# Queries and keys of a cross-attention layer transposed without padding and placed into the score operands by DMAs, in a program without a loop

## The chip, the cores and the metric

The kernel runs on one core of one Trainium2 chip. The metric is the device time of one execution in microseconds (us). A core has several engines, each with its own instruction queue: TensorE (PE in the profile, its weight loads PEld), VectorE (DVE), ScalarE (ACT), GpSimd (POOL) and SyncE (SP). Each works its own queue in order and waits for the others through semaphores. SP issues nearly all DMAs here.

## The reference

A batch has 128 tokens of width 256. Each of 16 batches goes through a cross attention with 32 heads of width 8 and a quantised feed-forward layer:

```python
x = x + xattn(layernorm(x), ctx, pos, pos, Wq, Wkv, Wout, bout)
x = x + ffn(layernorm(x), W1, b1, W2, b2, s_act1, s_act2)

q = (x @ Wq).reshape(b, n, 32, 8);  k, v = split(ctx @ Wkv)      # xattn
q, k = rope(q, pos), rope(k, ctx_pos)       # turns pairs (x1, x2) by angles
w = softmax(einsum('bqhd,bkhd->bhqk', q, k) / sqrt(8))
return einsum('bhqk,bkhd->bqhd', w, v).reshape(b, n, 256) @ Wout + bout
```

The feed-forward layer rounds its input, its weights and its hidden values (width 1024, after a ReLU) to 4 bits. The kernel keeps float32 accuracy in the scores by splitting a query or key into a rounded high part and a low rest; a score is then hi·hi + hi·lo + lo·hi, which are 24 rows of one contraction per head.

## The kernel before

The work is a software pipeline over batches. A *step* has eight *slots*, g = 0 to 7, and in step s stage n works on batch s - n: S_NORM (0), S_PROJ (1), S_STACK (2), S_MAX (3), S_ATT (4), S_OUT (5), S_FFN (6). There are 22 steps. The order of every engine's queue is written out by hand in its `body`. Steps 0 to 7 and 16 to 21 are straight code, and steps 8 to 15 are a loop of two steps. A slot of PE holds the scores of four heads for their maximum (`scores_for_max`, stage S_MAX), the scores of four heads of the batch before for the exponential (`scores_for_exp`, S_ATT), a weighing of values (`weigh_values`) and one or two other pieces of work, each in one of three shared PSUM banks (`ps_misc`; `claim` waits until the piece that had the bank before is emptied).

The part that the change touches:

- DVE multiplies the projected queries and keys by cosines and sines (`rope`, L796 and L801), and POOL adds the two into `rot` (L475).
- ACT writes the high part of each head twice into rows padded to 32 columns a head (`split_high`, L582: `q_rows`, `k_rows`), and POOL adds the low part (`split_low`, L483). The columns of four heads are 128 wide.
- PE transposes them four heads at a time, 8 + 8 transposes a batch in four pieces (`transpose_rows`: SQ0, SQ1, SK0, SK1), and ACT copies each piece out of PSUM, keys straight into `k_stack` (L601), queries into `q_comp` (L595).
- The queries of a group of four heads have to stand block-diagonally in `q_diag`: head j has its own rows and its own 128 columns, and the rest is zero. SP does this with four DMAs for each half of the groups (`place_queries`, L372).
- PE multiplies `k_stack` with `q_diag` in bf16 for the maxima. DVE reduces them (`maxima`, L810). PE transposes the maxima in two halves of 16 heads, DVE copies them to `mxT`, and SP places them in a row of `q_diag` that meets a row of -1 in `k_stack` (`place_maxima`, L380), so that the second scores, in float32r, come out with the maximum subtracted. First half in stage S_MAX, slot 4; second half in stage S_ATT, slot 1.

Both `k_stack` and `q_diag` have two buffers. `place_maxima`, `load_context` (L360) and `store` (L386, one store for two batches) stand in the same SP queue as `place_queries`.

## Time and profile before

| | |
|---|---|
| Time of an execution, median of 3 (lowest to highest) | 298.29 us (298.26 to 298.51) |
| Span of the profiled execution, first to last instruction | 296.1 us |
| PE busy | 250.3 us, 85% of the span, 2816 instructions |
| DVE busy | 223.3 us, 75% |
| ACT busy | 202.2 us, 68% |
| POOL busy | 128.1 us, 43% |
| Chain that ended last | PE 69%; issue 11%; DVE 10%; POOL 5%; ACT 4%; DMA 1% |
| Granted TensorE clock, mean | 0.943 of full speed |

The span is taken from one profiled execution, whose time as a whole is not listed; the median of the timed runs is 2.2 us above its span, which is what lies around the first and last instruction. The chain that ended last is followed back from the last instruction, at each step to what released it; "issue" is time in which the engine waited for nothing that the profile shows. Ends of matmuls are modelled, so that starts of neighbouring groups say more than their durations. DMA issues of SP are not counted as busy time, but the time that each held the queue is shown in a timeline of SP.

### The profile page before, as it was taken

The page shows a single profiled execution, that of the slowest core. Times are in us where ns is not written, and L with a number is a line of the kernel's source. Part 1 is how long each engine was busy: PE and PEld are TensorE (multiplying, and loading weights), DVE is VectorE, ACT ScalarE, POOL GpSimd, SP SyncE. Part 2 cuts the span into 40 slices and gives each one's busy share as a digit, 9 for nine tenths or more (in the row PEclk, how much of TensorE's full clock was granted, in tenths as well). Part 3 has the DMA queues.
Part 4 walks back from the last instruction along what each step waited for, and adds up shares of the span by engine and source line. Part 5 has one row for each costly group of instructions (what it writes and reads, how often), then busy time and mean ns, then how long its engine had stood idle before and what let it go on. Part 6 is the DMA issues. An engine that isn't in the chain of part 4 may idle for free.

```text
span 296.1 us, 8723 instructions
## 1 busy us (share of the span) xinstructions
PE 250.3 (85%) x2816; PEld 183.8 (62%) x2816; DVE 223.3 (75%) x570; ACT 202.2 (68%) x444; POOL 128.1 (43%) x266
## 2 busy tenths in 40 slices
PE   0056227899999999999999999999999999999653
PEld 0045126867767777777777777777777767665441
DVE  2977418797887979797979797979888877784441
ACT  3213025667679787878787878888887978679423
POOL 7625039444471717263635454445453451520110
PEclk9999557799999999999999999999999999999875
DMA  7921101252111113121211121112112111200101
GB/s 165 340 92 45 35 0 38 62 167 49 37 48 45 45 45 83 41 52 41 80 45 45 40 80 43 45 51 68 44 38 72 41 38 41 72 3 4 35 0 38
DMA packets 31786, 17.41 MB, mean 59 GB/s; under 512 B 6544, under 2 KB 31376, under 8 KB 31760
## 3 DMA queue, kind: packets, MB, share of 16 engines
q1 hardware_dynamic: 29696, 17.06, 21.8%
q10 hardware_dynamic: 2064, 0.02, 0.4%
q8 instruction: 15, 0.25, 0.3%
q14 instruction: 11, 0.09, 0.1%
HBM read 6.31 MB, written 2.10 MB: 28 GB/s over the span
## 4 chain that ended last, share of the span: by engine, by line
PE 69%; issue 11%; DVE 10%; POOL 5%; ACT 4%; DMA 1%; ACTq 0%; POOLq 0%; DVEq 0%
PE ps_misc L972 34%; PE ps_av L972 13%; PE ps_max L972 12%; PE ps_exp L972 9%; DVE turns L697 2%; ACT h_i L636 2%; DVE xn L867 1%; DMA q_diag<-mxT 1%; POOL rot L475 1%; DVE by_cos L796 1%; POOL q_rows L441 1%; DVE by_sin L801 1%; DVE xn L772 1%; POOL k_rows L442 1%; POOL rstd L515 1%
## 5 line engine op out<-in xcount | busy, mean ns | idle before, releaser
L810 DVE TENSOR_REDUCE mx<-ps_max 128x4 f32<-128x512 f32 x128 | 87.3, 686 | 30.0 <-PE ps_max L972 26.9
L607 ACT ACTIVATE expo<-ps_exp 128x512 f32<-128x512 f32 x128 | 77.7, 607 | 19.6 <-PE ps_exp L972 18.1
L972 PE MATMUL ps_exp<-q_diag,k_stack 128*128 128x512 f32 x128 | 60.3, 471 | 0.4 <-DMA q_diag<-mxT 0.4
L972 PE MATMUL ps_av<-expo,v_strip 128*32 128x128 f32 x1024 | 54.1, 285 | 0.0
L972 PE MATMUL ps_max<-k_stack,q_diag 96*128 96x128 bf16 (+1 forms) x512 | 52.9, 226 | 0.8 <-DVE mx L810 0.8
L636 ACT ACTIVATE h_i<-ps_misc,b1q,relu_scale 128x128 int16<-128x128 f32 x128 | 48.3, 470 | 2.5 <-PE ps_misc L972 2.5
L972 PEld LDWEIGHTS ps_max<-k_stack,q_diag 96*128 96x128 bf16 (+1 forms) x512 | 30.8, 99 | 24.5 <-issue 23.3
L500 POOL TENSOR_TENSOR v_strip<-v_comp,zeros 128x32 f32<-128x32 f32 x128 | 28.0, 256 | 19.4 <-PE ps_av L972 19.4
L972 PEld LDWEIGHTS ps_av<-expo,v_strip 128*32 128x32 f32 x1024 | 20.3, 108 | 21.8 <-issue 14.7
L483 POOL TENSOR_TENSOR q_rows<-rot,q_rows 128x256 f32<-128x256 f32 x16 | 11.6, 725 | 36.0 <-ACT q_rows L582 36.0
L972 PEld LDWEIGHTS ps_exp<-q_diag,k_stack 128*128 128x128 f32 x128 | 24.4, 190 | 1.5 <-issue 0.8
L468 POOL TENSOR_TENSOR rstd<-var,minus_half 128x1 f32<-128x1 f32 x16 | 8.9, 557 | 37.4 <-DVE var L766 37.4
L601 ACT CAST k_stack<-ps_misc 128x512 fp32r<-128x512 f32 x32 | 18.9, 590 | 8.6 <-PE ps_exp L972 5.3
L475 POOL TENSOR_TENSOR rot<-by_cos,by_sin 128x512 f32<-128x512 f32 x16 | 20.5, 1282 | 9.5 <-issue 6.9
L972 PE MATMUL ps_misc<-ident,q_rows 128*128 128x128 f32 x128 | 21.1, 291 | 1.8 <-POOL q_rows L483 1.8
L515 POOL TENSOR_TENSOR rstd<-var,minus_half 128x1 f32<-128x1 f32 x16 | 8.8, 549 | 30.8 <-DVE var L860 30.8
L595 ACT CAST q_comp<-ps_misc 128x512 fp32r<-128x512 f32 x32 | 19.1, 596 | 3.8 <-PE ps_misc L972 3.7
L972 PE MATMUL ps_misc<-xqT,w1T 128*128 128x128 bf16 x256 | 20.9, 229 | 0.7 <-ACT xqT L625 0.7
L972 PE MATMUL ps_misc<-ident,k_rows 128*128 128x128 f32 x128 | 19.9, 279 | 1.4 <-ACT v_comp L588 0.7
L972 PE MATMUL ps_misc<-w2T,hq 128*128 128x256 bf16 x128 | 17.7, 282 | 2.0 <-DVE hq L882 1.5
L483 POOL TENSOR_TENSOR k_rows<-rot,k_rows 128x256 f32<-128x256 f32 x16 | 11.7, 734 | 17.4 <-ACT k_rows L582 17.4
L582 ACT CAST q_rows<-rot 128x512 fp32r<-128x512 f32 x16 | 9.8, 613 | 13.1 <-POOL rot L475 13.1
(122 smaller groups left out, 514.3 us busy)
## 6 DMA issues: line engine op xcount, KB each, us to landing
q_diag<-q_comp SPq DMA_DIRECT2D x128, 64.0 KB, 2.0
w<-in_L_ffn_W_dram SPq DMA_DIRECT2D x2, 1024.0 KB, 8.2
...
q_diag<-mxT SPq DMA_DIRECT2D x32, 8.0 KB, 1.8
...
```

The source lines that it names most:

```text
L468: pool.tensor_tensor(rstd1[:, r, :], var1[:, r, :], minus_half[:, :], ALU.pow).then_inc(rstd1_ready, 1)
L475: pool.tensor_tensor(rot[:, r, :], by_cos[:, :], by_sin[:, :], ALU.add).then_inc(rot_ready, 1)
L483: pool.tensor_tensor(rows[:, r, :, at:at + HD], src, rows[:, r, :, 0:HD], ALU.subtract)\
L500: ins = pool.tensor_tensor(strips[:, s, :, 9 * s:9 * s + HD], vals, nothing, ALU.add)
L515: pool.tensor_tensor(rstd2[:, r, :], var2[:, r, :], minus_half[:, :], ALU.pow).then_inc(rstd2_ready, 1)
L582: act.copy(rows[:, :, 0:2, :] if n == 0 else rows[:, :, 0:3:2, :], src).then_inc(hi_ready, 1)
L595: act.copy(q_comp[:, r, 4 * half:4 * half + 4, :], src).then_inc(q_ready, 1)
L601: act.copy(k_stack[:, r, 4 * half:4 * half + 4, :], ps_misc[PIECE_BANK[(SK0, SK1)[half]]][:, :].rearrange("p (g t) -> p g t", g=4)).then_i ...
L607: act.activation(expo[:, g % EXPO, :], ps_exp[g % 2][:, :], ACT.Exp, scale=SCALE).then_inc(exp_done, 1)
L636: ins = act.activation(h_i[:, r, f, :], ps_misc[PIECE_BANK[(H0, H1)[half]]][:, 128 * c:128 * c + 128], ACT.Relu, bias=b1q[:, f:f + 1], sca ...
L810: dve.tensor_reduce(out=mx[:, r, 4 * g:4 * g + 4], in_=ps_max[g % 2][:, :].rearrange("p (h k) -> p h k", h=4), axis=AX.X, op=ALU.max).then ...
L972: return pe.matmul(out, lhsT, rhs, start=start, stop=stop, skip_group_check=True, **kw)
```

## The change

The queries and keys are no longer padded. The columns of Wq and of the key half of Wkv are reordered before the launch (`stack_order`), so that a transposed block of 128 columns of `rot` has its rows in the order that the score operands need. PE transposes `rot` itself, 4 transposes a batch in one piece (QKT) in slot 1. ACT writes the high part (`qk_hi`) and a full copy (`qk_full`), POOL subtracts (`qk_lo`). SP places everything: three DMAs for the keys and twelve for the queries, one for each part (high, high, low) and each of the four heads in a group. The operands have 96 rows in the order of the parts, and the row of maxima is row 96. `q_diag` and `k_stack` have three buffers; to make room, several tiles of the later stages reuse the memory of the unquantised weights (in the profile they are then called `w`). The DMAs of a batch count on one semaphore, `stacked`, and `scores_for_max` waits for all fifteen in slot 0.

The maxima are transposed and placed once a batch, in slot 0 of stage S_ATT. All later work, from `scores_for_exp` on, is three slots later (SHIFT = 3, `run_slots`; `st2` and `g2` are step and slot of that later part). The loop is gone: all 22 steps are straight code, with 3 slots more at the end. The order of the pieces and their banks is new. On DVE, `norm1` moves from slot `norm_at + 2` to `norm_at + 3`, and `rope` and `split_xT` to slots 4 and 3. POOL clears three buffers of `q_diag` in step 0.

```diff
-XT, SQ0, MX1, QK, SQ1, XQ, AT1, H0, SK0, MX0, AT2, VV, H1, WO, SK1, YY = range(16)
-PIECES = 16
-PIECE_BANK = (1, 2, 0, 1, 2, 0, 1, 0, 2, 1, 0, 2, 1, 0, 2, 0)
...
+MX, AT2, H1, WO, QKT, YY, XT, QK, XQ, AT1, H0, VV = range(12)
+PIECES = 12
+PIECE_BANK = (0, 1, 2) * 4
+SHIFT = 3
 EXPO = 4
...
+PART = 4 * HD
+NEG_ROW = 3 * PART
+STACK = 3
+PLACED = 16 * 15
 VREG = 3
...
+def run_slots(body):
+
+    for at in range(STEPS * GROUPS + SHIFT):
+        body(Step(at // GROUPS), at % GROUPS, Step((at - SHIFT) // GROUPS), (at - SHIFT) % GROUPS)
...
-        q_rows = sb("q_rows", [128, 2, HEADS, 32])
-        k_rows = sb("k_rows", [128, 2, HEADS, 32])
-        q_comp = sb("q_comp", [128, 2, GROUPS, 128], F32R)
-        k_stack = sb("k_stack", [128, 2, GROUPS, 128], F32R)
-        q_diag = sb("q_diag", [128, 2, GROUPS, 512], F32R)
+        qk_full = sb("qk_full", [128, 2, 2 * DIM])
+        qk_hi = sb("qk_hi", [128, 2, 2 * DIM], F32R)
+        qk_lo = sb("qk_lo", [128, 2, 2 * DIM], F32R)
+        k_stack = sb("k_stack", [128, STACK, GROUPS, 128], F32R)
+        q_diag = sb("q_diag", [128, STACK, 4, GROUPS, 128], F32R)
...
+            def stack_keys(st, part, rows):
+
+                at = st.ring(S_STACK, STACK)
+                dst = k_stack[PART * part:PART * part + PART, at, :, :].rearrange("p (g c) t -> p g (c t)", c=DC)
+                sp.dma_start(dst.bitcast(F32), rows[:, st.ring(S_STACK), DIM:2 * DIM].bitcast(F32)).then_inc(stacked[at], 16)
+
...
+            def spread_queries(st, part, rows):
+
+                at = st.ring(S_STACK, STACK)
                 for j in range(4):
...
+                    row = PART * part + HD * j
+                    dst = q_diag[row:row + HD, at, j, :, :].rearrange("p (g c) t -> p g (c t)", c=DC)
+                    src = rows[PART * j:PART * j + PART, st.ring(S_STACK), 0:DIM]
+                    sp.dma_start(dst.bitcast(F32), src.bitcast(F32)).then_inc(stacked[at], 16)
...
+            def stack(st):
+
+                st.wait(sp, qk_hi_ready, S_STACK, 1, 1)
+                st.wait(sp, exp_scores, S_STACK, GROUPS, GROUPS - STACK * GROUPS)
+                if st.s == S_STACK:
+                    sp.wait_ge(zeros_ready, 3)
+                stack_keys(st, 0, qk_hi)
+                stack_keys(st, 2, qk_hi)
+                spread_queries(st, 0, qk_hi)
+                spread_queries(st, 1, qk_hi)
+                st.wait(sp, qk_lo_ready, S_STACK, 1, 1)
+                stack_keys(st, 1, qk_lo)
+                spread_queries(st, 2, qk_lo)
+
+            def place_maxima(st):
+
+                at = st.ring(S_ATT, STACK)
+                st.wait(sp, mxT_ready, S_ATT, 1, 1)
+                dst = q_diag[NEG_ROW:NEG_ROW + 1, at, :, :, :].rearrange("o j g t -> o (j g) t")
+                sp.dma_start(dst.bitcast(F32), mxT[:, st.ring(S_ATT), :].bitcast(F32)).then_inc(neg_placed[at], 16)
 
             def store(st):
 
                 st.wait(sp, y_ready, S_FFN, 1, 1)
-                pair = st.value(1, (st.s - S_FFN) // 2)
+                pair = st.batch(S_FFN) // 2
                 sp.dma_start(out_pairs[pair], y[:, :, :]).then_inc(stored, 16)
...
+                if st.has(S_ATT):
+                    place_maxima(st)
                 if st.has(S_NORM) and st.s > 1:
                     load_context(st)
-                if not st.looped and st.s in (2, 4):
+                if st.s in (2, 4):
                     load(3 if st.s == 2 else 4)
-                if st.has(S_ATT):
-                    place_maxima(st, 1, S_ATT)
                 if st.has(S_STACK):
-                    place_queries(st, 0)
-                if st.has(S_MAX):
...
-            def split_low(st, n):
-
-                r = st.ring(S_PROJ)
-                rows, at = (q_rows, k_rows)[n], (16, 8)[n]
-                st.wait(pool, hi_ready, S_PROJ, 2, n + 1)
-                src = rot[:, r, n * DIM:(n + 1) * DIM].rearrange("p (h d) -> p h d", d=HD)
-                pool.tensor_tensor(rows[:, r, :, at:at + HD], src, rows[:, r, :, 0:HD], ALU.subtract)\
-                    .then_inc(lo_ready, 1)
+            def split_low(st):
+
+                r = st.ring(S_STACK)
+                st.wait(pool, qk_full_ready, S_STACK, 1, 1)
+                st.wait(pool, qk_hi_ready, S_STACK, 1, 1)
+                wait_stacked(pool, st)
+                pool.tensor_tensor(qk_lo[:, r, :], qk_full[:, r, :], qk_hi[:, r, :].bitcast(F32), ALU.subtract)\
+                    .then_inc(qk_lo_ready, 1)
 
...
+                prev = Step(st.s - 1)
+                if st.has(S_STACK):
+                    split_low(st)
+                if prev.has(S_OUT):
+                    norm2(prev)
+                    if prev.s == S_OUT:
+                        pool.wait_ge(bias_ready, 2)
...
+                    for r in range(STACK):
+                        clear_diagonal(r)
...
-                act.copy(q_comp[:, r, 4 * half:4 * half + 4, :], src).then_inc(q_ready, 1)
-
-            def copy_keys(st, half):
+                st.wait(act, qkT_in_psum, S_STACK, 1, 1)
+                wait_stacked(act, st)
+                act.copy(qk_hi[:, r, :], ps_misc[PIECE_BANK[QKT]][:, :]).then_inc(qk_hi_ready, 1)
+
+            def copy_qk(st):
                 r = st.ring(S_STACK)
-                st.wait(act, k_in_psum, S_STACK, 2, half + 1)
-                st.wait(act, exp_scores, S_STACK, GROUPS, 4 * half + 4 - 2 * GROUPS)
-                act.copy(k_stack[:, r, 4 * half:4 * half + 4, :],
-                         ps_misc[PIECE_BANK[(SK0, SK1)[half]]][:, :].rearrange("p (g t) -> p g t", g=4)).then_inc(k_ready, 1)
+                st.wait(act, qk_lo_ready, S_STACK, 1, -1)
+                act.copy(qk_full[:, r, :], ps_misc[PIECE_BANK[QKT]][:, :]).then_inc(qk_full_ready, 1)
...
+                cos_b = bcast(bcast(cos8[:, b, :, :].rearrange("p f c -> p (f c)"), 1, 2 * GROUPS), 3, 4)
+                dve.tensor_tensor(by_cos[:, :].rearrange("p (g d j) -> p g d j", d=HD, j=4),
+                                  ps.rearrange("p (g d j) -> p g d j", d=HD, j=4), cos_b, ALU.mult).then_inc(rope_terms, 1)
...
+                if g == norm_at + 3 and st.has(S_NORM):
+                    norm1(st)
...
-            def transpose_rows(st, piece, rows, in_psum, ready, half):
-                ps, r = claim(st, piece), st.ring(S_STACK)
-                st.wait(pe, lo_ready, S_STACK, 2, ready)
-                for g in range(4):
-                    h = 4 * (4 * half + g)
-                    ins = transpose(ps[:, 128 * g:128 * g + 128], rows[:, r, h:h + 4, :].rearrange("p h c -> p (h c)"),
-                                    ident[:, :])
-                ins.then_inc(in_psum, 1)
+            def transpose_qk(st):
+                ps, r = claim(st, QKT), st.ring(S_STACK)
+                st.wait(pe, rot_ready, S_STACK, 1, 1)
+                for n in range(4):
+                    ins = transpose(ps[:, 128 * n:128 * n + 128], rot[:, r, 128 * n:128 * n + 128], ident[:, :])
...
             def scores_for_max(st, g):
 
-                r = st.ring(S_MAX)
-                if g % 4 == 0:
-                    st.wait_dma(pe, diag_placed[g // 4], S_MAX, 64)
-                    st.wait(pe, k_ready, S_MAX, 2, g // 4 + 1)
+                at = st.ring(S_MAX, STACK)
+                if g == 0:
+                    st.wait_dma(pe, stacked, S_MAX, PLACED)
                 st.wait(pe, max_done, S_MAX, GROUPS, g - 1)
...
-            def transpose_maxima(st, half, stage, piece):
-                ps, r = claim(st, piece), st.ring(stage)
-                st.wait(pe, max_done, stage, GROUPS, 4 * half + 4)
-                transpose(ps[0:16, 0:128], mx[:, r, 16 * half:16 * half + 16], ident[:, :]).then_inc(mx_in_psum, 1)
+            def transpose_maxima(st):
+                ps, r = claim(st, MX), st.ring(S_ATT)
+                st.wait(pe, max_done, S_ATT, GROUPS, GROUPS)
+                transpose(ps[0:HEADS, 0:128], mx[:, r, :, :].rearrange("p j g -> p (j g)"), ident[:, :]).then_inc(mx_in_psum, 1)
 
             def scores_for_exp(st, g):
 
-                r = st.ring(S_ATT)
-                if g % 4 == 0:
-                    st.wait_dma(pe, neg_placed[g // 4], S_ATT, 16)
+                at, rows = st.ring(S_ATT, STACK), slice(0, NEG_ROW + 1)
+                if g == 0:
...
+                if g == 0 and st.has(S_ATT):
+                    transpose_maxima(st)
+                if g2 == 5 and st2.has(S_OUT):
+                    transpose_attn(st2)
+                if g2 == 6 and st2.has(S_OUT):
+                    project_out(st2)
+                if g == 3 and st.has(S_PROJ):
+                    transpose_x(st)
+                if g2 == 3 and st2.has(S_OUT):
+                    transpose_av(st2)
+                if st2.has(S_ATT):
+                    scores_for_exp(st2, g2)
+                if g2 == 5 and st2.has(S_FFN):
+                    hidden(st2, 1, H1)
...
+def stack_order(name, a):
+
+    if name == 'L0_xattn_Wq':
+        return a.reshape(DIM, 4, DC, 4, HD).transpose(0, 2, 3, 4, 1).reshape(DIM, DIM)
+    if name == 'L0_xattn_Wkv':
+        keys = a[:, :DIM].reshape(CTX, 4, DC, 4, HD).transpose(0, 2, 3, 4, 1).reshape(CTX, DIM)
+        return np.concatenate([keys, a[:, DIM:]], axis=1)
+    return a
 
```

The queue of SP. Before, one step of the straight part (step 7). `mxT` are the maxima, and `out_dram` is the output:

```order
L380 DMA q_diag<-mxT 1x16x128 [waits mxT_ready]
L372 DMA q_diag<-q_comp 32x4x128 [waits exp_scores,q_ready]
L372 DMA q_diag<-q_comp 32x4x128 x3
L380 DMA q_diag<-mxT 1x16x128 [waits mxT_ready]
L372 DMA q_diag<-q_comp 32x4x128 [waits exp_scores,q_ready]
L372 DMA q_diag<-q_comp 32x4x128 x3
L386 DMA out_dram<-y 128x2x256 [waits y_ready]
```

The same place of SP's queue in the changed kernel, step 7 and behind it the first instruction of step 8:

```order
L377 DMA q_diag<-mxT 1x32x128 [waits mxT_ready]
L341 DMA c_in<-in_ctx_dram 128x128 [waits xT_in_psum]
L347 DMA k_stack<-qk_hi 32x4x256 [waits exp_scores,qk_hi_ready]
L347 DMA k_stack<-qk_hi 32x4x256
L356 DMA q_diag<-qk_hi 8x4x256 x8
L347 DMA k_stack<-qk_lo 32x4x256 [waits qk_lo_ready]
L356 DMA q_diag<-qk_lo 8x4x256 x4
L383 DMA out_dram<-w 128x2x256 [waits y_ready]
L377 DMA q_diag<-mxT 1x32x128 [waits mxT_ready]
```

Fifteen DMAs stand where eight stood, and the maxima of the next step come right behind the store.

PE before, slot 4 of step 7:

```order
L972 MATMUL ps_max<-k_stack,q_diag 128x128 [waits max_done,k_ready,diag_placed_hi0]
L972 MATMUL ps_max<-k_stack,q_diag 128x128 x3
L972 MATMUL ps_misc<-ident,k_rows 128x128 [waits lo_ready,q_ready]
L972 MATMUL ps_misc<-ident,k_rows 128x128 x3
L972 MATMUL ps_exp<-q_diag,k_stack 128x512 [waits exp_done,neg_placed_hi1]
L972 MATMUL ps_misc<-ident,mx 16x128 [waits max_done,attn_ready]
L972 MATMUL ps_av<-expo,v_strip 32x128 [waits exp_done]
L972 MATMUL ps_av<-expo,v_strip 32x128 x3
```

PE in the changed kernel, slot 0 of a step, with the wait for the fifteen DMAs at its head:

```order
L935 MATMUL ps_max<-k_stack,q_diag 128x128 [waits max_done,stacked2]
L935 MATMUL ps_max<-k_stack,q_diag 128x128 x3
L935 MATMUL ps_misc<-ident,mx 32x128 [waits max_done,attn_ready]
L935 MATMUL ps_misc<-ident,attn 128x128 [waits attn_ready,relu_done]
L935 MATMUL ps_misc<-ident,attn 128x128
L935 MATMUL ps_exp<-q_diag,k_stack 128x512 [waits exp_done]
L935 MATMUL ps_misc<-xqT,w1T 128x128 [waits xqT_ready,v_copied]
L935 MATMUL ps_misc<-xqT,w1T 128x128 x7
```

PE in the changed kernel, from the last product of the feed-forward layer in slot 2 (`w2T`) to the first scores of the next batch for the exponential in slot 3, which wait for the placed maxima:

```order
L935 MATMUL ps_misc<-w2T,w 128x256 [waits hq_ready]
L935 MATMUL ps_misc<-w2T,w 128x256 x3
L935 MATMUL ps_av<-expo,v_strip 32x128 [waits exp_done]
L935 MATMUL ps_av<-expo,v_strip 32x128 x3
L935 MATMUL ps_max<-k_stack,q_diag 128x128 [waits max_done]
L935 MATMUL ps_max<-k_stack,q_diag 128x128 x3
L935 MATMUL ps_misc<-ident,xn 128x128 [waits c_loaded0,xn_ready,x2_ready]
L935 MATMUL ps_misc<-ident,xn 128x128
L935 MATMUL ps_misc<-ident,c_in 128x128
L935 MATMUL ps_exp<-q_diag,k_stack 128x512 [waits exp_done,neg_placed0]
```

Before, the last product of a batch stood in slot 7 and the placed maxima were waited for in slots 0 and 4; now these two stand in neighbouring slots.

## Rows read from the trace of the kernel before

**Rows 1.** Windows: length, busy us (x instructions) by engine, PEclk, DMA share, GB/s.

```profile
24.00:43.00 19.00, 6.71 (x38) 5.03 (x36) 8.63 (x15) 3.79 (x8) 4.73 (x13) 0.67 0.13 31
...
103.29:218.75 115.46, 115.46 (x1394) 86.02 (x1393) 99.00 (x264) 96.05 (x217) 55.02 (x121) 1.00 0.21 52
```

**Rows 2.** Timeline of PE, slots 4 to 7 of step 7: start, us, what.

```profile
103.13 0.60 PE L972 MATMUL ps_misc<-ident,k_rows 128*128 128x128 f32 x4
103.48 0.48 PE L972 MATMUL ps_exp<-q_diag,k_stack 128*128 128x512 f32 x1
103.80 0.27 PE L972 MATMUL ps_misc<-ident,mx 128*16 128x128 f32 x1
104.01 0.43 PE L972 MATMUL ps_av<-expo,v_strip 128*32 128x128 f32 x8
104.36 0.41 PE L972 MATMUL ps_max<-k_stack,q_diag 96*128 96x128 bf16 x4
...
105.06 0.28 PE L972 MATMUL ps_misc<-wkv_hi,xT_hi 128*128 128x256 f32 x1
...
105.41 0.62 PE L972 MATMUL ps_misc<-xqT,w1T 128*128 128x128 bf16 x8
106.32 0.41 PE L972 MATMUL ps_max<-k_stack,q_diag 96*128 96x128 bf16 x4
...
107.55 0.60 PE L972 MATMUL ps_misc<-ident,k_rows 128*128 128x128 f32 x4
108.07 0.43 PE L972 MATMUL ps_av<-expo,v_strip 128*32 128x128 f32 x8
108.43 0.41 PE L972 MATMUL ps_max<-k_stack,q_diag 96*128 96x128 bf16 x4
108.65 0.48 PE L972 MATMUL ps_exp<-q_diag,k_stack 128*128 128x512 f32 x1
108.97 1.05 PE L972 MATMUL ps_misc<-w2T,hq 128*128 128x256 bf16 x8
...
110.31 0.41 PE L972 MATMUL ps_max<-k_stack,q_diag 96*128 96x128 bf16 x4
```

**Rows 3.** Timeline of PE, first scores of steps 4, 17 and 18.

```profile
55.18 1.06 PE L972 MATMUL ps_max<-k_stack,q_diag 96*128 96x128 bf16 x8
...
240.21 0.41 PE L972 MATMUL ps_max<-k_stack,q_diag 96*128 96x128 bf16 x4
...
253.57 0.41 PE L972 MATMUL ps_max<-k_stack,q_diag 96*128 96x128 bf16 x4
...
265.00 0.49 PE L972 MATMUL ps_exp<-q_diag,k_stack 128*128 128x512 f32 x1
```

**Rows 4.** Timeline of SP: start, us that the issues held the queue, what.

```profile
24.93 5.29 SPq L372 DMA_DIRECT2D q_diag<-q_comp  x8
30.27 0.59 SPq L360 DMA_DIRECT2D c_in<-in_ctx_dram  x1
...
109.21 2.54 SPq L372 DMA_DIRECT2D q_diag<-q_comp  x4
111.79 0.59 SPq L386 DMA_DIRECT2D out_dram<-y  x1
113.05 0.35 SPq L360 DMA_DIRECT2D c_in<-in_ctx_dram  x1
```

**Rows 5.** Instructions on the tile q_diag: duration ns min/median/max, first and last start.

```profile
L380 SPq DMA_DIRECT2D q_diag<-mxT x32: 502/569/602, 53.1 to 267.1; - x32
...
DMA to landing us min/median/max: 1.8/2.0/3.7
```

**Rows 6.** The page's costliest groups: ACT's copy of four transposes, mean ns.

```profile
L595 ACT CAST q_comp<-ps_misc 128x512 fp32r<-128x512 f32 x32 | 19.1, 596 | 3.8 <-PE ps_misc L972 3.7
```

**Rows 7.** Groups by line: DVE's output of a batch.

```profile
L889 DVE SCALAR_TENSOR_TENSOR y<-ps_misc,h_scale,x_b 128x256 f32<-128x256 f32 x16 | 7.8, 484 | 4.6 <-PE ps_misc L972 3.9
```

**Rows 8.** Timeline of all engines: POOL's rotation of batch 1.

```profile
40.06 1.25 POOL L475 TENSOR_TENSOR rot<-by_cos,by_sin 128x512 f32<-128x512 f32 x1 [6.89 <-issue]
```

492 lines of the change are left out of this document (193 added, 299 removed).

## Prediction

> **What bounds the kernel now.** I read the page's shares first. PE is busy for 85% of the span, and holds 69% of the chain that ended last; the span's ends are where it is not busy. The windows then show that in the middle it is busy without a gap: 115.46 of 115.46 us, at the full clock, against 99.00 for DVE and 96.05 for ACT [rows 1]. Eight steps begin alike there, and a step lasts (240.21 - 110.31) / 9 = 14.43 us [rows 2, 3]. So what PE no longer does is gained, until another engine or a queue needs more than a step. DVE needs 99.00 / 8 = 12.4 us of a step and ACT 12.0. The engine that counts as nothing in these views is SP. Its timeline [rows 4] shows that four placing DMAs hold its queue for 2.54 us, and that the next issue begins 2.58 us after the first: 0.645 us for each. Eight of them cost 5.2 us of a step, in two halves, and PE never waits for one.
>
> **PE's work per step.** Twelve transposes go. Four take 103.48 - 103.13 = 0.35 us in one place and 108.07 - 107.55 = 0.52 in another [rows 2], 0.11 us each in the mean: -1.3 us. One of two transposes of maxima goes (104.01 - 103.80 = 0.21). The rest is moved, not changed: the contraction of the scores gets 96 or 97 rows instead of 96 or 128, and the number of columns that stream through is the same. PE would need 14.43 - 1.3 - 0.2 = 12.9 us. DVE loses one copy and keeps about 12.2, and ACT loses six passes of about 0.6 us [rows 6] for two. If nothing else came up, the nine full steps alone would bring 14 us.
>
> **Loop, shift, set-up.** The loop's turns leave no gap in [rows 1], so I take nothing for removing it. The three slots at the end are without scores for the maxima; they cost 4.6 us, as worked out below. POOL clears two more buffers in step 0, and saves the padding; its rotation of batch 0 waits for DVE anyway. I put nothing for both.
>
> **The queue of SP is what I expect to set the time.** Follow a step of the changed kernel from its first scores, T. Slot 0 holds what slot 5 held (104.36 to 106.32, 1.96 us [rows 2]) without the values' projection (105.41 - 105.06 = 0.35) and with the maxima (0.21): 1.82 us. Slot 1 holds exactly the pieces of the old slot 6, whose transposes ended 108.07 - 106.32 = 1.75 after its start: the four transposes end at T + 3.57, and slot 2 begins at T + 3.93 (slot 6: 2.11). ACT has its exponential behind it, copies `qk_hi` in 0.6 us [rows 6] and is done at about T + 4.3. SP waits also for the last exponential scores of three batches back, which stand in slot 2: they start at T + 3.93 + (108.65 - 108.43 = 0.22) and take 0.48 [rows 2]. So the first of fifteen DMAs is issued at T + 4.65. The low part, which the last five need, comes from ACT's second copy (T + 4.9) and a POOL pass of 1.25 us like the rotation [rows 8], at T + 6.2, well before its turn.
>
> The price of an issue: the trace of before has no transfer of these shapes. The nearest rows are 0.645 us for 32 x 4 x 128 [rows 4] and 0.569 + 0.04 = 0.61 for the small transfer of the maxima [rows 5], which moves an eighth of the bytes: the size hardly matters. Between them I take 0.645 for the three key DMAs and 0.62 for the twelve of queries. The last issue then begins 3 x 0.645 + 11 x 0.62 = 8.8 us after the first, and lands 2.0 us later [rows 5]. That is T + 4.65 + 8.8 + 2.0 = T + 15.45. PE waits for all fifteen at the head of the next step, and needed only 12.9 us to come there. It stands still for 2.5 us, and the next step's transposes begin after that: the delay is not absorbed, it is the period. The third buffer does not help, because transposes, DMAs and first use lie in two neighbouring steps. The bounds: above, 0.66 us for an issue, as in the first eight (30.27 - 24.93 = 5.34 [rows 4]), which makes a step 16.0 us. Below, 0.35 + 0.04 us, as the context's load when nothing is just ahead of it [rows 4]; the fifteenth then lands at T + 12.1 and is hidden.
>
> The Trainium skill speaks against this price: "DMA: Bandwidth & Descriptors", section "Anatomy of one DMA — SWDGE (gpsimd) path" (written for DMAs that GpSimd issues), puts the sequencer's dispatch at about 50 ns and most of a DMA's 2 us behind the last byte, and the section "Issuing engines are not separate DMA queues" calls the time to initiate a DMA usually small. By its 50 ns all fifteen would land at about T + 7.4. The trace disagrees with 0.645 us of queue for each, and I go by the trace; landing in 2.0 us agrees.
>
> **The store's wait, every second step.** The store of two batches waits for y. Its last product is now in slot 2 of the next step: it starts at T + 3.93 + 0.54 and takes 1.05 us, DVE's output 0.48 [rows 7], so y is ready at T + 6.1. Queued behind the store on SP are the maxima (wanted by PE in slot 3, at about T + 6.3), the context, and all fifteen DMAs. Store, maxima and context take 3 x 0.62 = 1.9 us (the store 0.59 [rows 4]). The maxima are issued at T + 6.7 and land 1.8 us later [rows 5], at T + 8.5: PE waits 2.2 us in slot 3. The first of fifteen is issued at T + 8.0 instead of T + 4.65, so the step lasts 8.0 + 8.8 + 2.0 = 18.8 us; the stall in slot 3 disappears in that. The stores of steps 7, 9, 11, 13 and 15 do this to steps 8, 10, 12, 14 and 16.
>
> **The sum.** Batch 1 is rotated until 41.3 us [rows 8]. DVE now does its rope after scaling the weights, which I give up to 2 us, and transposes and copy at the low clock take 1.2: its DMAs start at 44.5 and land at 55.3, when step 4 begins (55.6 before, the second half of the eight in [rows 3]). Steps 4, 5 and 6 have fewer pieces ahead of the transposes: without exponential scores, feed-forward and output projection I take 2.7, 3.2 and 4.1 us in place of 4.65. With 10.8 each, step 7 begins at 97.7. One step of 15.45: step 8 at 113.1 (110.3 before). One of 18.8: step 9 at 131.9. Four pairs of 34.25: step 17 at 268.9 (240.2 before [rows 3]). One of 15.45: step 18 at 284.4 (253.6 before). Step 18 has no transposes and no stacking but waits 2.2 us for the maxima behind the last such store: 13.3 us, to 297.7 (265.0 before). From there the old kernel took 296.1 - 265.0 = 31.1 us, and the new one adds the three slots: 1.82 + 2.11 + 1.88 - 3 x 0.22 - 0.52 = 4.6. The span is 333.4 us. With the 2.2 us that lie around it (298.29 - 296.1) the time is 335.6 us: 12% slower.
>
> **Rivals.**
> - *The issues are cheap and the fifteen DMAs are hidden* (the skill's rule, or the 0.35 us of [rows 4]). For it speaks that the transfers of queries have only 32 runs each, a quarter of before, and that the DMA engines are busy for 0.21 of the time [rows 1]. Against it: the transfer of the maxima has even fewer and held the queue for 0.569 us in the median of 32. A step is then 12.9 us, and the step after a store 14.6 to 14.8, because the maxima behind the store remain late (1.8 us of landing after T + 6.1). Steps 4 to 8 come 3 to 7 us earlier, the pair lasts 27.5 us for 28.9, and the three slots cost 4.6: 290 us, to 294 at 0.39 us for an issue. This is the other side: it turns at about 0.43 us for an issue, above which the pair with the store costs more than is gained.
> - *Only the fifteen DMAs delay, the store's wait costs nothing*: if y were ready before SP is through, all steps would last 15.45 us. Five steps lose 3.35 us less and step 18 2.2: 335.6 - 19 = 317 us. The order of the instructions speaks against it, since SP is through with step 7 at T + 4.65 + 9.4 = T + 14.1, before y's step begins.
> - *DVE or POOL becomes the bound* when PE sheds work: DVE's 12.2 us are below 12.9, and its waits for PE would shrink. It could make 13.2 us of 12.9, and matters only beside the first rival.
> - *The clock falls* in the new gaps. It was 0.67 where PE worked for 6.71 of 19.00 us [rows 1]; here it would work for 12.9 of 15.45. At the lower of its two levels (1.2 instead of 2.4 GHz) PE would be the bound again at up to 25 us a step, above 400 us.
>
> **Chances and range.** The forecast has 0.69, the cheap issues 0.14 (split into 0.12 faster and 0.02 within the bound), the free store 0.14, the clock 0.03. About 0.2% is what a measurement of this kernel can tell from no change; only the first rival reaches there. So faster 0.12, same 0.02, slower 0.86. For the forecast alone: issues of 0.60 to 0.66 us move a step by 0.3 us down and 0.6 us up, 14 steps by 4 and 8 us; a start of the DMAs 0.4 us earlier or later does 6; a landing up to 0.4 us later another 6. That is 322 to 348. The range reaches down to 311 to hold the second rival and leaves out the first.
>
> **What would show it.** PE's scores for the maxima (`ps_max`) wait for a DMA of `q_diag` or `k_stack` once a step, about 2.5 us after steps without a store and about 3.7 us at the end of those behind a store (18.8 less the 15.1 that PE needs with its stall in slot 3). The chain that ended last shifts from PE to SP's issues and landing DMAs. SP's timeline shows fifteen issues in 9.4 us. `ps_exp` waits for the maxima's DMA in steps 8, 10, ... by about 2 us. Transposes of `rot` are 64 in all, in place of 256. The steps alternate near 15.4 and 18.8 us. The forecast is wrong if an issue holds SP's queue for 0.4 us or less, or if first scores don't wait for DMAs; the sum is wrong in size if the start of the fifteen lies elsewhere than 4.65 and 8.0 us into a step.

## The result: 31% slower, and the profile after

| | before | after | forecast |
|---|---|---|---|
| median, us | 298.4 (298.3 to 300.1, 4 runs) | 392.8 (389.8 to 395.9, 4 runs) | 335 (311 to 348) |
| span of the profiled execution, us | 296.1 | 389.2 | 333.4 |
| PE busy | 85% | 69% | |

The ratio of the times is 1.313 (95% interval 1.304 to 1.321); it leaves out the run of 395.9 us, and every ratio below leaves out runs that lie more than 1.5% above the fastest of the same kernel, while the medians hold all runs. The direction was forecast, the time lies far above the range. First the page of the changed kernel: PE's share of the span, the granted clock in 40 slices, and the chain that ended last.

```profile
PE 267.8 (69%) x2608; PEld 190.4 (49%) x2608; DVE 227.5 (58%) x554; ACT 174.0 (45%) x380; POOL 127.1 (33%) x249
...
PEclk9999995887978887898698788968896889689995
...
SPq 39%; PE 26%; issue 12%; DMA 11%; DVE 8%; POOL 3%; ACT 1%; ACTq 0%; POOLq 0%; DVEq 0%
```

SP's queue leads the chain with 39%, where PE had 69% before. New is the third row: the clock is no longer full in the middle (1.00 in [rows 1]), and is 0.851 in the mean. The waits say who waits for whom (total, times, longest, in us):

```profile
PE ps_max L935 <- DMA q_diag<-qk_lo: 54.7, 15, 6.0
...
PE ps_exp L935 <- DMA q_diag<-mxT: 14.9, 6, 3.5
```

Both waits are the forecast ones: first scores for the maxima wait 15 times for the last query DMAs, and exponential scores 6 times for the maxima behind a store. Now one step without a store ahead of it, in which PE's two ends are 174.50 - 156.09 = 18.41 us apart (15.45 forecast). PE first:

```profile
156.09 0.40 PE L935 MATMUL ps_max<-k_stack,q_diag 96*128 96x128 bf16 x4 [1.95 <-DMA q_diag<-qk_lo]
...
159.18 0.41 PE L935 MATMUL ps_misc<-wout_hi,attnT_hi 128*128 128x256 f32 x1
...
160.46 0.66 PE L935 MATMUL ps_misc<-ident,rot 128*128 128x128 f32 x4
...
174.50 0.61 PE L935 MATMUL ps_max<-k_stack,q_diag 96*128 96x128 bf16 x4 [3.64 <-DMA q_diag<-qk_lo]
```

Then SP's queue in the same step (start, how long the issues held it):

```profile
162.17 1.24 SPq L347 DMA_DIRECT2D k_stack<-qk_hi  x2
163.46 5.83 SPq L356 DMA_DIRECT2D q_diag<-qk_hi  x8
169.33 0.59 SPq L347 DMA_DIRECT2D k_stack<-qk_lo  x1
169.96 2.81 SPq L356 DMA_DIRECT2D q_diag<-qk_lo  x4
```

The first of fifteen is issued at T + 6.08 (4.65 forecast), the last one at about 172.1, 9.93 us after it (8.8 forecast), and PE starts on it 2.4 us later (2.0 forecast). The sum 6.08 + 9.93 + 2.4 is the step. The row at 159.18 tells why the start is late: this product of 128x256 takes 0.41 us where the same form takes 0.28 at full clock [rows 2]. The first scores behind the stall still have the duration of full clock (0.40 us at 156.09); PE's clock then stood at the lower of its two levels from about 157.6 us until the transposes began at 160.46. Over the whole step the granted clock was 0.90, and over the next one 0.77.

The next step stands behind a store and takes 195.85 - 174.50 = 21.35 us (18.8 forecast):

```profile
181.83 0.40 SPq L383 DMA_DIRECT2D out_dram<-w  x1
182.27 0.57 SPq L377 DMA_DIRECT2D q_diag<-mxT  x1
182.89 0.58 SPq L341 DMA_DIRECT2D c_in<-in_ctx_dram  x1
183.58 1.25 SPq L347 DMA_DIRECT2D k_stack<-qk_hi  x2
```

```profile
184.45 0.80 PE L935 MATMUL ps_exp<-q_diag,k_stack 97*128 97x512 f32 x1 [2.15 <-DMA q_diag<-mxT]
...
195.85 0.40 PE L935 MATMUL ps_max<-k_stack,q_diag 96*128 96x128 bf16 x4 [1.49 <-DMA q_diag<-qk_lo]
```

Store, maxima, context and stack stand in the order that was forecast, and the stall in slot 3 has the forecast size (2.15 for 2.2). That the sizes agree so well is partly luck: the store held the queue for less than forecast (0.44 us to the next issue, for 0.62), and the maxima took longer to land (2.1 us in the median, for 1.8). The start is at T + 9.08 in place of 8.0. A pair of steps lasts 39.76 us where 34.25 were forecast.

The start is late too. Step 4 begins at 62.65 instead of 55.3, and most of that comes from a place at which I had put nothing. DVE, then POOL:

```profile
7.95 11.54 DVE L663 CAST red<-turns 128x64 f32<-128x64 int32 x1
19.52 0.23 DVE L664 SCALAR_TENSOR_TENSOR red<-red,ang 128x64 f32<-128x64 f32 x1
```

```profile
9.02 10.42 POOL L439 MEMSET q_diag<- 128x4096 int32 x3
```

A conversion of 64 columns that takes 0.20 us elsewhere shows 11.54 us. It begins beside POOL's subtraction for `wkv_lo` (7.82 to 9.08) and ends as POOL's three clears end. The first norm is behind the rope tables now.

### The profile page after: what moved, and what is told of

It reads as the page before. It is cut to its first block, busy times and chain, and to the rows that moved or that the text cites. A ratio compares the mean times of both kernels' runs of the same rounds, so it can differ in the third digit from the quotient of the medians.

```text
span 389.2 us, 7534 instructions
## 1 busy us (share of the span) xinstructions
PE 267.8 (69%) x2608; PEld 190.4 (49%) x2608; DVE 227.5 (58%) x554; ACT 174.0 (45%) x380; POOL 127.1 (33%) x249
## 2 busy tenths in 40 slices
DMA packets 27701, 21.74 MB, mean 56 GB/s; under 512 B 6544, under 2 KB 27280, under 8 KB 27664
## 4 chain that ended last, share of the span: by engine, by line
SPq 39%; PE 26%; issue 12%; DMA 11%; DVE 8%; POOL 3%; ACT 1%; ACTq 0%; POOLq 0%; DVEq 0%
SPq L356 29%; PE ps_misc L935 13%; DMA q_diag<-qk_lo 9%; SPq L347 7%; PE ps_max L935 5%; PE ps_exp L935 4%; PE ps_av L935 4%; DVE red L663 3%; SPq L377 1%; DMA pos_sb<-in_fside_BxSx_dram 1%; DVE w L856 1%; SPq L341 1%; DMA q_diag<-mxT 1%; SPq L383 1%; DVE w_i L698 1%
## 5 line engine op out<-in xcount | busy, mean ns | idle before, releaser
L935 PE MATMUL ps_max<-k_stack,q_diag 96*128 96x128 bf16 x512 | 59.4, 247 | 56.5 <-DMA q_diag<-qk_lo 54.7
L935 PE MATMUL ps_exp<-q_diag,k_stack 97*128 97x512 f32 x128 | 69.4, 542 | 14.9 <-DMA q_diag<-mxT 14.9
L935 PEld LDWEIGHTS ps_max<-k_stack,q_diag 96*128 96x128 bf16 x512 | 34.9, 108 | 86.0 <-DMA q_diag<-qk_lo 58.6
L469 POOL TENSOR_TENSOR qk_lo<-qk_full,qk_hi 128x512 fp32r<-128x512 f32 x16 | 20.3, 1272 | 129.0 <-ACT qk_full L575 129.0
L609 ACT ACTIVATE w<-ps_misc,b1q,relu_scale 128x128 int16<-128x128 f32 x128 | 48.0, 461 | 4.9 <-PE ps_misc L935 4.8
L935 PEld LDWEIGHTS ps_exp<-q_diag,k_stack 97*128 97x128 f32 x128 | 28.7, 224 | 17.5 <-DMA q_diag<-mxT 16.3
L935 PEld LDWEIGHTS ps_misc<-xqT,w1T 128*128 128x128 bf16 x256 | 19.0, 118 | 7.0 <-issue 5.4
L935 PE MATMUL ps_misc<-w2T,w 128*128 128x256 bf16 x128 | 17.6, 283 | 2.7 <-ACT w L609 2.7
L935 PEld LDWEIGHTS ps_misc<-w2T,w 128*128 128x128 bf16 x128 | 11.6, 101 | 6.7 <-ACT w L609 3.1
L935 PE MATMUL ps_misc<-ident,rot 128*128 128x128 f32 x64 | 12.5, 330 | 2.8 <-POOL rot L461 2.8
```

Source lines behind the costliest of these rows:

```text
L469: pool.tensor_tensor(qk_lo[:, r, :], qk_full[:, r, :], qk_hi[:, r, :].bitcast(F32), ALU.subtract)\
L609: ins = act.activation(h_i[:, r, f, :], ps_misc[PIECE_BANK[(H0, H1)[half]]][:, 128 * c:128 * c + 128], ACT.Relu, bias=b1q[:, f:f + 1], sca ...
L935: return pe.matmul(out, lhsT, rhs, start=start, stop=stop, skip_group_check=True, **kw)
```

## The experiments

Step lengths below are read from PE's first scores, as above. "Before" ran beside every kernel, at 297.8 to 298.8 us.

| kernel (no ratio where a part of the work is left out) | us, median (4 to 10 runs) | ratio to before |
|---|---|---|
| changed kernel | 392.8 | 1.313 |
| store behind the next stacking | 375.5 | 1.260 [1.256, 1.264] |
| half the bytes | 387.3 (380.9 to 391.1) | |
| eleven DMAs | 341.0 (337.3 to 345.0) | |
| PE kept busy | 373.7 | 1.256 [1.249, 1.263] |
| spread clears | 391.2 | 1.312 [1.308, 1.317] |
| late store, busy PE, spread clears | 348.8 | 1.173 [1.168, 1.177] |
| an extra step between stacking and use | 299.2 | 1.003 [1.001, 1.006] |
| POOL issues the low part | 364.7 | 1.222 [1.216, 1.228] |
| the same, behind the second norm | 305.3 | 1.018 [1.013, 1.024] |
| three queues | 308.6 | 1.030 [1.025, 1.036] |
| before, loop written out | 298.4 | 0.999 [0.997, 1.002] |
| before, reduction moved | 301.4 | 1.008 [1.004, 1.011] |

**The store's wait** (e1). The call moves from the step of its batch to the next one, behind its stacking:

```diff
-                if st.has(S_FFN) and st.ring(S_FFN) == 1:
-                    store(st)
+                prev = Step(st.s - 1)
+                if prev.has(S_FFN) and prev.ring(S_FFN) == 1:
+                    store(prev)
...
+            store(Step(STEPS - 1))
```

> Undoes one wait of the changed kernel: the store of a pair of outputs, which waits for y, is issued behind the stacking of the next step instead of ahead of it. My theory (the fifteen issues and their landing are the period; the store's wait delays their start in every second step) expects the first stacking DMA at about 6.1 us into every step, no stall of the first exponential scores for the maxima, pairs of 2 x 18.4 = 36.8 us in place of 39.8, and 392.8 - 5 x 3.0 - 2.9 = about 375 us. The rival that the period of a pair is set by PE's lower clock alone expects no change, 390 to 396 us. Slower than 396 would mean that the later store makes DVE's output wait.

Measured: 375.5 us, and no stall for the maxima. Steps 13 and 14 last 37.4 us (266.60 - 229.21) instead of 40.8, and the five pairs from step 8 to 18 last 38.1 in the mean instead of 40.5. The store's wait is shown, at 2.4 us a pair, less than the 3.0 expected; another 5.2 us are won behind the start of step 18, where 2.9 were expected. In steps 13 and 14 the first DMA was issued at T + 6.9 and T + 6.0, not at T + 6.1 in both. The clock does not recover alike each time: products of 128x256 still took 0.41 us at T + 4.2 in the first step, and 0.28 us from T + 3.5 on in the second.

**Bytes or issues** (e2, e3).

```diff
-...rearrange("p (g c) t -> p g (c t)", c=DC)
+...rearrange("p (g c) t -> p g (c t)", c=DC)[:, :, 0:128]
```

> The twelve query DMAs of a step are as many as in the changed kernel, but each moves only the first half of its 256 columns; the scores are therefore computed on queries that are half zeros, and the output isn't the reference's. The theory that SP's queue is held for a fixed time by each issue expects 0.66 to 0.67 us an issue as before, and 388 to 394 us. The rival that bytes or descriptors behind the issue set its time or its landing expects issues of 0.35 to 0.5 us or a landing 1 us shorter: a step 1 to 3.5 us shorter, 345 to 378 us.

The query issues of this kernel (min, median, max in ns), then the end of one chain and the scores that wait for it:

```profile
L356 SPq DMA_DIRECT2D q_diag<-qk_hi x128: 659/672/987, 31.1 to 329.3; - x128
```

```profile
210.74 2.81 SPq L356 DMA_DIRECT2D q_diag<-qk_lo  x4
```

```profile
214.92 0.52 PE L935 MATMUL ps_max<-k_stack,q_diag 96*128 96x128 bf16 x4 [3.23 <-DMA q_diag<-qk_lo]
```

The changed kernel has 659/672/1388: half the bytes, in as many packets (27701 in both), do not change what an issue costs. They do change the landing a little. The last issue begins at 210.74 + 2.81 - 0.67 = 212.88, and PE starts 2.04 us behind it; in fifteen steps it is 2.05 to 2.08, where the changed kernel has 2.34 to 2.41. Fourteen steps of 0.33 us are 4.6 us, about what the median is lower (387.3 for 392.8), a difference that the spread of the runs (380.9 to 391.1, and 389.8 to 395.9) would not settle by itself. The measured 387.3 lies just under the 388 to 394 that were expected, and far above the rival's 345 to 378.

```diff
-                spread_queries(st, 2, qk_lo)
...
-PLACED = 16 * 15
+PLACED = 16 * 11
```

> Leaves out the four DMAs of the queries' low part (and so that part of the scores' product): eleven stacking DMAs a step in place of fifteen. The theory of the issue chain expects the last issue 4 x 0.70 = 2.8 us earlier in each of 14 steps, 392.8 - 39 = 354 us, and down to 340 if PE's clock falls less with the shorter gap. The rival that landing or the waits for the store and the maxima set the period, and not the number of issues, expects less than 10 us, 383 to 393 us.

341.0 us (337.3 to 345.0): four issues fewer bring 52 us, at the lower end of what was expected. SP in one step without a store, which starts at 203.02 and whose successor starts at 217.49:

```profile
207.63 1.23 SPq L347 DMA_DIRECT2D k_stack<-qk_hi  x2
208.91 5.76 SPq L356 DMA_DIRECT2D q_diag<-qk_hi  x8
214.71 0.59 SPq L347 DMA_DIRECT2D k_stack<-qk_lo  x1
```

The step is 14.47 us: 4.61 to the first issue, 7.08 to the last, 2.78 to the end. Of the 3.9 us won, 2.85 are issues, and 1.47 are the earlier start that the smaller clock loss gives, less 0.4 of a longer landing: the last DMA is now one of keys, with 128 KB in place of 32.

**The clock** (e4). Sixteen products in PE's gap:

```diff
+                st.wait(pe, max_done, S_MAX, GROUPS, g - 1)
                 if g == 0:
+                    for _ in range(16):
+                        mm(ps_max[0][:, 0:512], w1T[:, 0, 0, :], ...)
                     st.wait_dma(pe, stacked, S_MAX, PLACED)
-                st.wait(pe, max_done, S_MAX, GROUPS, g - 1)
```

> Sixteen products of 128 x 512 (bf16, result overwritten) are put on PE behind the last scores of a step, ahead of its wait for the stacking DMAs, so that PE isn't still there; all else as in the changed kernel. My theory of the second loss (PE's granted clock falls behind the stall, and the transposes and so the first issue come 1.4 us late) expects a granted clock near 1.0 in the middle, the first stacking issue at 4.7 us into a step without a store behind it in place of 6.1, steps about 1.4 us shorter, 392.8 - 14 x 1.4 = about 373 us. The rival that the lower clock costs nothing beside the issue chain expects 390 to 396 us. Slower than 400 would mean that the products themselves outlast the gap.

373.7 us, as expected. Windows over four steps, of the changed kernel first and then of this one (length, busy times, and after POOL the granted clock):

```profile
235.68:317.24 81.56, 64.51 (x644) 46.44 (x645) 48.53 (x124) 41.33 (x92) 26.08 (x55) 0.83 0.15 50
```

```profile
225.88:301.85 75.97, 70.47 (x708) 46.03 (x709) 47.98 (x124) 40.46 (x92) 26.11 (x55) 0.96 0.17 53
```

With more work on PE the four steps take 5.6 us less. The first DMA of the step at 225.88 is issued at 230.50, T + 4.62. So the 4.65 of the forecast is right for a full clock, and the missing 1.4 us a step are the clock's.

**The start** (e5). SP then waits for one clear at a time instead of all three.

```diff
-                if st.s == S_STACK:
-                    sp.wait_ge(zeros_ready, 3)
+                if st.s < S_STACK + STACK:
+                    sp.wait_ge(zeros_ready, st.s - S_STACK + 1)
...
-                if st.s == 0:
-                    for r in range(STACK):
-                        clear_diagonal(r)
+                if st.s < STACK:
+                    clear_diagonal(st.s)
```

> POOL clears one buffer of the query operand in each of the steps 0, 1 and 2, in place of all three in step 0; all else as in the changed kernel. My theory of the late start (POOL's three clears hold DVE's rope tables up for 11.5 us, so that the first norm and the first scores come 7 us late) expects the conversion of the turns with less than 5 us of idle time ahead of it, the first scores of step 4 near 55 us in place of 62.7, and 392.8 - 7 = about 386 us. The rival that the start waits for the loads or for the rope tables' own work, whatever POOL does, expects 390 to 396 us.

The conversion is rid of its 11.54 us, though operations of DVE still stretch beside POOL, the first two beside its subtractions (that for `wq_lo` ends at 7.91) and the third beside the one clear left. DVE, then POOL:

```profile
6.82 1.14 DVE L662 CAST red<-turns 128x64 f32<-128x64 int32 x1
7.99 1.22 DVE L663 SCALAR_TENSOR_TENSOR red<-red,ang 128x64 f32<-128x64 f32 x1
...
9.76 2.87 DVE L669 TENSOR_SCALAR red<-red 128x64 f32<-128x64 f32 x1
```

```profile
7.87 1.26 POOL L435 TENSOR_TENSOR wkv_lo<-wkv,wkv_hi 128x512 fp32r<-128x512 f32 x1
9.07 3.51 POOL L439 MEMSET q_diag<- 128x4096 int32 x1
```

Step 4 begins at 57.07, 5.6 us earlier. The time is 391.2 us, though, no measurable gain: the lead is 5.4 us at step 9 and 0.3 at step 12. Between these two the granted clock was 0.83, against 0.87 in the changed kernel. Why it fell more there isn't settled by one profile each. The run with three edits bears on it.

**Three losses at once** (e9: the edits of e1, e4 and e5).

> Three of the edits together: the store behind the next stacking, sixteen products on PE ahead of its wait, clears spread over three steps. If the three losses that I name are separate, a step is 4.7 + 9.9 + 2.4 = 17.0 us throughout: 375.5 (late store alone) - 19 (clock) - 7 (clears) = about 349 us, down to 335 if the pairs gain as one. If two of them are the same loss seen twice, the sum comes to 360 us or more. What then is left over the 298.3 us of before is the chain of fifteen issues alone.

348.8 us. A step, from 178.04 to 195.50, is even and without the clock's loss:

```profile
178.04 0.40 PE L936 MATMUL ps_max<-k_stack,q_diag 96*128 96x128 bf16 x4
...
195.50 0.40 PE L936 MATMUL ps_max<-k_stack,q_diag 96*128 96x128 bf16 x4 [0.64 <-DMA q_diag<-qk_lo]
```

```profile
182.64 1.92 SPq L347 DMA_DIRECT2D k_stack<-qk_hi  x2
184.61 5.76 SPq L356 DMA_DIRECT2D q_diag<-qk_hi  x8
190.41 0.59 SPq L347 DMA_DIRECT2D k_stack<-qk_lo  x1
191.05 2.81 SPq L356 DMA_DIRECT2D q_diag<-qk_lo  x4
```

4.60 + 10.55 + 2.31 = 17.46 us. The three together bring 44.0 us. One by one they bring 17.3 + 19.1 + 1.6 = 38.0. The 6 us more are about what the start won in the trace of e5 (5.6); that they are the same microseconds is not shown. So the total agrees with the forecast of this run partly by luck, since its sum put 7 us on the clears alone. What is left over before, 50 us, is put down to the chain of fifteen issues, and the next kernel tests that.

**The chain taken apart** (e6). `S_MAX` is two steps behind `S_STACK` instead of one, with four operand buffers; late store and spread clears as above:

```diff
-S_NORM, S_PROJ, S_STACK, S_MAX, S_ATT, S_OUT, S_FFN = range(7)
+S_NORM, S_PROJ, S_STACK, S_MAX, S_ATT, S_OUT, S_FFN = 0, 1, 2, 4, 5, 6, 7
```

> One more step lies between the stacking of a batch and its first scores (four buffers of the operands, the values kept two steps longer, other tensors laid over dead ones to make room), and the store and the clears are moved as in the experiments with a late store and with spread clears. The fifteen DMAs of a step are all there. My theory that they cost time only because issue and landing lie between transposes and first use of neighbouring steps expects SP to need 15 x 0.66 + 0.57 + 0.58 + 0.3 = 11.4 us of a step, below PE's 12.9, no wait of first scores for a DMA, a full clock, steps of 12.9 to 13.3 us, and 280 to 292 us: under the kernel before. The rival that SP's queue or the DMA engines bound the kernel in themselves expects steps above 14.4 us and more than 310 us.

299.2 us: 94 us less with all fifteen DMAs in place, but not under the kernel before. Windows over eight steps, then PE's first slot of one:

```profile
118.14:226.60 108.46, 107.19 (x1293) 76.65 (x1289) 95.95 (x253) 79.88 (x185) 52.96 (x111) 1.00 0.23 75
```

```profile
143.22 0.40 PE L936 MATMUL ps_max<-k_stack,q_diag 96*128 96x128 bf16 x4
143.82 0.27 PE L936 MATMUL ps_misc<-ident,mx 128*32 128x128 f32 x1 [0.19 <-DVE mx L777]
...
145.33 0.40 PE L936 MATMUL ps_max<-k_stack,q_diag 96*128 96x128 bf16 x4
```

In these eight steps no DMA is waited for, and PE is busy 99% at a full clock. But a step lasts 13.6 us (156.84 - 143.22), not 12.9. The slot with the maxima's transpose takes 2.11 us, where I had worked out 1.82. The transpose stands right behind the first scores of the next batch now and waits for DVE's reduction of the last ones, and the 0.21 us for the second transpose did not come back: in the slot at 112.01 of before, it was followed by the exponential scores 0.02 us later. With 13.6 us the gain on a step of 14.43 is 0.8. From the first scores of the first batch to those of the last it adds up to 12.1 us; but the first scores come 8.1 us later (51.5 for 43.5), with the extra step, and behind the last ones lie 5.5 us more, with the three slots. DVE, busy for 95.95 of the 108.46 us, is not the bound that the third rival of the prediction feared.

**Two and three queues** (e8, e10, e11). POOL issues the five DMAs of the low part, right behind its subtraction:

```diff
-                st.wait(sp, qk_lo_ready, S_STACK, 1, 1)
-                stack_keys(st, 1, qk_lo)
-                spread_queries(st, 2, qk_lo)
...
+                    pool.dma_start(dst.bitcast(F32), src.bitcast(F32)).then_inc(by, 16)
```

> The five DMAs of the low part are issued by POOL behind its subtraction, with a semaphore of their own; SP issues the ten others; all else as in the changed kernel. The theory that one queue's issues in a row are the period expects SP's last issue 9 x 0.67 = 6.0 us after its first and its landing at 6.1 + 6.0 + 2.4 = 14.5 us into the step in place of 18.4: 392.8 - 14 x 3.5 = about 344 us, if an issue of POOL costs no more than 1.2 us. The rival that the DMA engines and not the issues are slow, or that POOL's issues cost 2 us each, expects 375 us or more.

Only 28 us came, not 49. Only one step still waited noticeably for the stack. The maxima behind the store cost 23.4 us in six waits, and in nine of the steps PE waited for `xq`:

```profile
268.96 0.27 PE L948 MATMUL ps_misc<-ident_bf,xq 128*128 128x128 bf16 x2 [2.32 <-DVE xq L855]
```

```profile
263.27 0.60 POOL L478 DMA_DIRECT2D k_stack<-qk_lo  x1 [0.30 <-POOL qk_lo L470]
263.86 2.16 POOL L483 DMA_DIRECT2D q_diag<-qk_lo  x4
266.04 0.57 POOL L514 TENSOR_TENSOR rstd<-var,minus_half 128x1 f32<-128x1 f32 x1
```

The issues hold POOL for 2.76 us, and the inverse deviation of the second norm is behind them, on the path to `xq`. The next kernel turns that order round, and has the late store and the spread clears:

```diff
                 if prev.has(S_OUT):
                     norm2(prev)
+                if st.has(S_STACK):
+                    stack_low(st)
```

> The split over two queues once more, now with the wait removed that took its gain: POOL issues its five DMAs behind the inverse deviation of the second norm instead of ahead of it; the store is behind the next stacking, the clears are spread over three steps. All fifteen DMAs are there, without an extra step. My theory expects SP's ten DMAs to land 4.7 + 5.9 + 2.1 = 12.7 us into a step, POOL's five at 6.6 + 2.3 + 3.3 = 12.2, both before PE's 13.6, so no wait of PE for them; a full clock; first scores at about 42 us, steps of 13.6 us as with the extra step, 42 + 199 + 46 + 2 = 289 us: 3% under the kernel before. The rival that POOL's queue, once busy, holds up the rotation or the values, or that the two queues slow each other, expects steps of 15 us or more and over 310 us.

305.3 us: both waits are gone, but the rest fell short. Steps last 13.9 us in the mean, with waits up to 2.3 us for SP's ten DMAs, and step 3 begins at 46.1, not 42. The landing is longer in some steps:

```profile
148.44 5.77 SPq L358 DMA_DIRECT2D q_diag<-qk_hi  x8
```

```profile
157.13 0.40 PE L955 MATMUL ps_max<-k_stack,q_diag 96*128 96x128 bf16 x4 [1.33 <-DMA q_diag<-qk_hi]
```

SP's last issue begins at 153.54, and PE starts 3.6 us behind it. Over the eleven steps that wait it is 2.3 to 3.6 us, where it was 2.3 to 2.4 with SP alone.

ACT then takes the two key DMAs, and the reduction of the weights' maximum over partitions comes a step earlier, with POOL's second and third clears and the value strips moved behind it. The control is the kernel before with only the reduction and the strips moved:

```diff
-                stack_keys(st, 0, qk_hi)
-                stack_keys(st, 2, qk_hi)
...
+                    act.dma_start(dst.bitcast(F32), ...).then_inc(stacked_k[at], 16)
```

```diff
-                if not st.looped and st.s == 2:
+                if False:
                     pool.wait_ge(wmax_ready, 2)
...
                 if not st.looped and st.s == 1:
+                    pool.wait_ge(wmax_ready, 2)
+                    pool.partition_all_reduce(wmax_all[:, :], ...)
...
+                if not st.looped and st.s == 2:
                     fill_strips()
```

> Goes on from the split over two queues, which waited for SP's ten DMAs by 0.2 to 2.3 us a step and ran steps of 14.0 us: ACT issues the two key DMAs of the high part behind its copies, so that SP issues eight, and POOL reduces the weights' maximum over partitions at the end of step 1, ahead of the second and third clear and of the value strips. Expected: last landing of SP at 4.7 + 4.7 + 2.1 = 11.5 us into a step, no wait of first scores for a DMA, steps of 13.6 us (-0.4 x 13 = -5 us), first scores 4 to 5 us earlier than 46.1: 305.3 - 10 = about 295 us, 1% under the kernel before. The rival that ACT's issues delay its exponentials as much as they relieve SP, or that the start waits for something else, expects 300 to 306 us.

> A control: the kernel before with only the new place of the reduction over partitions (end of step 1, the value strips in step 2), nothing of the change. If the start is bound by that reduction (5.6 us ahead of it, 6.9 behind it on POOL), first scores come 3 to 5 us earlier than 43.5 and the time is 294 to 296 us: then what the three queues gain by it isn't theirs. If not, 298 us or more, since the low part of batch 0 now waits behind it.

Both missed. The control is slower by 0.8%, and POOL's rows show why. The reduction with the time around it takes about as long wherever it stands (12.9 us in the kernel before, 13.75 here), and a norm that stood ahead of it is now behind it. Before, then the control:

```profile
26.61 0.55 POOL L468 TENSOR_TENSOR rstd<-var,minus_half 128x1 f32<-128x1 f32 x1 [0.71 <-DVE var L766]
```

```profile
29.55 0.37 POOL L552 PARTITION_ALL_REDUCE wmax_all<-wmax  x1 [5.78 <-issue]
37.53 0.59 POOL L468 TENSOR_TENSOR rstd<-var,minus_half 128x1 f32<-128x1 f32 x1 [7.60 <-issue]
```

In the kernel with three queues the low part of the first batch stands behind the reduction: POOL issues it from 36.6 us on instead of 28.8, and the first scores come at 53.3 us instead of 46.1. From there to the first scores of the last batch the three queues are 3.1 us faster than the two (205.8 for 208.9), which the late start more than uses up. The steps in the middle last 14.0 us, not 13.6. PE still waits for SP's DMAs in seven steps, by 0.2 to 1.3 us, though SP issues only eight, and for ACT's copy of the values in ten, by up to 0.3 us. The issues, then one chain and the scores behind it:

```profile
L361 SPq DMA_DIRECT2D q_diag<-qk_hi x128: 659/672/902, 23.1 to 255.5; - x128
L489 POOL DMA_DIRECT2D q_diag<-qk_lo x64: 544/547/644, 37.5 to 254.6; - x64
```

```profile
237.01 5.69 SPq L361 DMA_DIRECT2D q_diag<-qk_hi  x8
```

```profile
245.89 0.40 PE L969 MATMUL ps_max<-k_stack,q_diag 96*128 96x128 bf16 x4 [0.21 <-DMA q_diag<-qk_hi]
```

SP's last issue begins at 242.03, and PE starts 3.9 us behind it (3.4 to 4.0 in the seven steps). The chain of eight is 1.4 us shorter than one of ten, and the longer landing takes most of that back.

**The loop** (e7): the kernel before, every step written out.

```diff
 def run_steps(eng, body, hold=None):
+    for s in range(STEPS):
+        body(Step(0, s, False))
+    return
```

> One part of the change alone: the kernel before with its loop written out as a straight program, nothing else. My step, which put nothing for the loop, expects 298.3 us, within 0.3%. The rival that a loop's turns or a longer program's instruction fetches cost something expects 1 to 3 us more or less.

298.4 us, ratio 0.999 [0.997, 1.002]. Nothing for the loop was right.

## Why the prediction was right and wrong

- *SP's queue sets the period*: right, and shown from three sides. Fewer issues (e3), other queues (e10) and distance between issue and use (e6) each take the greater part of the loss away; half the bytes (e2) take some 5 of it, by a shorter landing. The first rival, cheap issues, falls with the 0.67 us of a query issue.
- *The price of the fifteen*: mostly 9.9 to 10.5 us from first to last, not 8.8. The key DMAs at 0.64 were right. The query DMAs take 0.672 + 0.04 = 0.71, not 0.62. I had chosen between the two nearest rows, and the truth lay above both. It is 1.1 us a step or more, 16.7 us over the 14 steps from 4 to 17.
- *The landing*: 2.3 to 2.4 us from the last issue to PE's start, not 2.0. Some 5 us in all.
- *T + 4.65*: right at a full clock (4.60 to 4.62 in e4 and e9), 6.08 in the changed kernel. The step that failed is "the clock falls" as an all-or-nothing rival. I priced PE as bound at the lower level and gave the forecast itself nothing. In truth stalls of the size that I did forecast (2.5 and 3.7 us, measured mostly 2 to 4) go with a granted clock of 0.83. PE runs at the lower level for some 3 us of a step, and its transposes stand on the path. e4 measures 19.1 us for it, the largest term that was left out.
- *The store's wait*: right in mechanism, place and the stall of slot 3 (2.15 for 2.2). e1 puts it at 17.3 us, where the forecast had 19. That agreement is partly luck: the forecast had 3.35 us a pair and 2.2 at the end, and measured are 2.4 and 5.2. The second rival (the store is free) falls.
- *The set-up at nothing*: wrong. Step 4 began at 62.65, 7.3 us late, and spreading POOL's three clears, which stood beside DVE's rope tables, takes 5.6 of that away in the trace of e5. The cover that I named, that the rotation waits for DVE anyway, was what the clears held up. The trace of before already had it in small, one table operation of DVE stretched beside POOL's one clear (8.97 to 12.47), and I didn't look there:

```profile
7.88 4.65 DVE L697 TENSOR_SCALAR turns<-ang 128x64 int32<-128x64 f32 x1
12.56 0.20 DVE L698 CAST red<-turns 128x64 f32<-128x64 int32 x1
```

- *PE needs 12.9 us*: wrong by 0.7, shown by e6. It did not matter in the changed kernel, where PE waits. It is part of why e6 does not beat the kernel before; nine full steps at 12.9 us would be 6 us shorter.
- *The range*: its terms were issues (8 us), start (6) and landing (6) upward. Added up they reach 356 us, not 348, and downward 326, not 322. Neither upper end comes near 392.8, since the clock was in no term.

The excess of 55.8 us in the span is 7.3 up to step 4, 43.9 from there to step 18 and 4.6 behind it. Read step by step from the rows of SP and PE, the 43.9 are 21.9 of first issues that come late, 16.7 of longer chains and 5.3 between the last issue and PE's start. The 19 us of e4 are most of the first. The remaining 3 us, and how the clock's loss spreads over single steps, aren't settled.
